# Scores from stacked high and low parts, and three norms in a written-out order

## What is computed

```python
# after the experts (L0_ffn), y is the attention's normed output
z = _layer_norm(y + _moe(y, ...), g2, be2)        # norm 0, with gain and shift
x = x + _layernorm(z)                             # norm 1
# second attention (L1_attn), called on _layernorm(x)
xn = _ln(_layernorm(x), g1, b1)                   # norm 2
q = _lin(xn, Wq, bq).reshape(b, n, 16, 8) / sqrt(8)
k = _lin(xn, Wk, bk).reshape(b, n, 16, 8)
score = softmax(einsum('bihd,bjhd->bhij', q, k))
v = _lin(xn, Wv, bv).reshape(b, n, 8, 8)
out = einsum('bhij,bjrd->bihrd', score, v)        # 8 values per head
comp = softmax(concat([qv, out]) @ Ws.T + bs, axis=3)
out = (comp * out).sum(axis=3)                    # 128 features per token
```

## Time and profile before

| | us |
|---|---|
| median of 3 runs (1008.1 to 1018.52) | 1008.54 |
| profiled execution | 1008.61 |
| its span, first to last instruction | 1006.9 |
| PE busy | 742.9 (74%) |
| DVE busy | 589.5 (59%) |
| ACT busy | 446.8 (44%) |
| POOL busy | 84.6 (8%) |

### The profile page before, as it was taken

How to read it: one execution, slowest core, us unless ns; L and a number is a source line. 1 busy time by engine, 2 the same in 40 slices (tenths; PEclk the granted TensorE clock), 3 DMA queues, 4 the chain that set the end, 5 groups by cost and what they waited for, 6 DMA issues and landing times. The chain is left out here.

```text
span 1006.9 us, 15707 instructions
## 1 busy us (share of the span) xinstructions
PE 742.9 (74%) x5853; PEld 608.8 (60%) x5853; DVE 589.5 (59%) x1330; ACT 446.8 (44%) x920; POOL 84.6 (8%) x96
## 2 busy tenths in 40 slices
PE   3993869998932695518940479999999974759986
PEld 2443769995432475418840347888888864538765
DVE  4119999983484363413327543777777657575574
ACT  3332526453534454203534614555555533446554
POOL 0002203000001101061420020000000001000000
PEclk9996757697955788557985569999999986869989
DMA  5200260005001000021020030000000000000000
GB/s 166 33 0 1 41 105 1 1 3 220 26 1 64 1 1 1 1 68 46 31 63 0 0 118 1 2 2 1 0 1 1 2 1 1 0 1 1 1 22 21
DMA packets 27457, 26.43 MB, mean 26 GB/s; under 512 B 17424, under 2 KB 25488, under 8 KB 26624
## 3 DMA queue, kind: packets, MB, share of 16 engines
q1 hardware_dynamic: 26144, 22.99, 8.0%
q0 software_dynamic: 1248, 2.57, 0.8%
HBM read 20.32 MB, written 5.23 MB: 25 GB/s over the span
## 5 line engine op out<-in xcount | busy, mean ns | idle before, releaser
L2201 PE MATMUL PS<-VXT,PT 128*128 128x73 f32 (+1 forms) x1024 | 126.6, 277 | 4.8 <-ACT PT L2225 4.8
L2201 PEld LDWEIGHTS PS<-VXT,PT 128*128 128x128 f32 x1024 | 119.7, 192 | 17.0 <-issue 12.3
L2312 DVE TENSOR_REDUCE MX<-PS 128x2 f32<-128x512 f32 x128 | 81.7, 686 | 47.5 <-PE PS L2164 46.8
L2225 ACT ACTIVATE PT<-PS 128x512 f32<-128x512 f32 x128 | 68.6, 597 | 47.4 <-PE PS L2169 47.4
L2161 PE MATMUL PS<-Q,KZ 32*128 32x256 f32 x512 | 76.8, 397 | 0.0
L2164 PE MATMUL PS<-KZ,Q 32*128 32x256 f32 x512 | 72.8, 409 | 1.9 <-DVE MX L2312 1.7
L2169 PE MATMUL PS<-MR,SEL 32*128 32x256 f32 x256 | 58.8, 462 | 0.0
L2238 ACT ACTIVATE UB<-PS 128x292 f32<-128x292 f32 x64 | 26.6, 415 | 52.8 <-PE PS L2201 52.8
L2164 PEld LDWEIGHTS PS<-KZ,Q 32*128 32x128 f32 x512 | 45.1, 190 | 5.3 <-DVE MX L2312 4.1
L404 PE MATMUL PS<-XT,WT 128*128 x96 | 42.3, 595 | 1.0 <-ACT XT L290 1.0
L2161 PEld LDWEIGHTS PS<-Q,KZ 32*128 32x128 f32 x512 | 38.8, 184 | 5.7 <-issue 0.8
(11 more groups left out here) (465 smaller groups left out, 1778.3 us busy)
## 6 DMA issues: line engine op xcount, KB each, us to landing
PB<-in_pb SPq DMA_DIRECT2D x1, 5016.0 KB, 17.7
PB<-in_pd SPq DMA_DIRECT2D x1, 2888.0 KB, 9.8
X<-in_x SPq DMA_DIRECT2D x2, 1024.0 KB, 4.8
X<-fir_rows SPq DMA_DIRECT2D x2, 1024.0 KB, 6.5
TR<-fir_rows SPq DMA_DIRECT2D x2, 1024.0 KB, 8.7
PA<-in_pa SPq DMA_DIRECT2D x1, 1731.0 KB, 8.5
PC<-in_pc SPq DMA_DIRECT2D x1, 1560.0 KB, 6.4
by_expert<-ZERO_ SPq DMA_DIRECT2D x1, 1483.5 KB, 15.7
```

What stands on the lines that cost most here:

```text
L2201: last = nc.tensor.matmul(PS[:, UM.bank(n), col:col + VX], PT[:, k % 4, c, f * P:(f + 1) * P], v, start=(c == 0), stop=(c == 1))
L2225: nc.scalar.activation(PT[:, k % 4, :, :], PS[:, UM.bank(n), :].rearrange("p (c q) -> p c q", c=2), ACT.Exp).then_inc(c_act, 1)
L2312: nc.vector.tensor_reduce(MX[:, :, k], PS[:, UP_.bank(n), :].rearrange("p (f q) -> p f q", f=2), AX.X, ALU.max, negate=True).then_inc(p_dv ...
```

## The change

1. **Queries and keys as high and low parts.** The projection is taken in two halves of another precision: ACT writes the fp32r-rounded high part (`high_parts`, two applies), DVE the rest (`low_parts`, two operations). For each group of 32 rows the four planes (query high, query low, key high, key low) are spread by 32 DMAs of 32 KB from SP (`spread`) into Q4 and K4, so that one head has, under one another in 32 rows, 8 rows each of high and low queries against high and low keys. One fp32r matmul over 32 rows then adds all four products. Q4 and K4 are kept three times, HALVES once. The weights' columns are laid out as "p (j d s)", and bias columns are permuted by a matmul with PERM.
2. **The attention's turns.** The hardware loop is gone: all turns are written out. The projection of batch b+2 moves to iteration 0 of turn b, right behind its scores, in the third slot of the maxima's rotation (SPLIT_BANK, bank 2), and the low parts to DVE's iteration 1. PE's next use of that bank (the sixth maximum, in `scores(2)`) waits for both parts. The maxima of the next turn wait for the spread of their batch, and ACT's high parts for the spread before.
3. **The applies into OB** leave norm 2; the 16 of them stand behind the high parts of batch 1, before turn 0.
4. **The three norms** follow an order written out per engine, one (k, g) at a time; `end(k, g)` now ends with `begin(k + 1, g)`. Batch 0 is split there, between `turned(1)` and `apply(2, 2)` on ACT and behind `middle(2, 3)` on DVE, and SP's part of the block ends with `spread(0)`.
5. At the block's beginning DVE makes the permuted bias columns behind SEL and PE multiplies them with PERM, between its gain columns and the product with BD; some bias arithmetic after the fold gets shorter.

The diff, cut to its core:

```diff
+        def high_parts(act, bank, b):
+            act.wait_ge(split_full, b + 1)
+            if b:
+                arrived(act, b - 1)
+            for s_ in range(2):
+                nc.scalar.activation(HALVES[:, 2 * s_, :], bank[:, s_ * L:(s_ + 1) * L], ACT.Identity,
+                                     bias=BS[:, s_:s_ + 1]).then_inc(split_high, 1)
+
+        def low_parts(dve, bank, b):
+            dve.wait_ge(split_high, 2 * b + 2)
+            for s_ in range(2):
+                nc.vector.scalar_tensor_tensor(out=HALVES[:, 2 * s_ + 1, :], in0=bank[:, s_ * L:(s_ + 1) * L],
+                                               scalar=BS[:, s_:s_ + 1], in1=HALVES[:, 2 * s_, :], op0=ALU.add,
+                                               op1=ALU.subtract).then_inc(split_low, 1)
+
+        def spread(sp, b):
+            sp.wait_ge(split_high, 2 * b + 2)
+            sp.wait_ge(split_low, 2 * b + 2)
+            for to, plane_of in ((Q4, lambda c: c // 2), (K4, lambda c: 2 + c % 2)):
+                for g in range(4):
+                    for c in range(4):
+                        at = 32 * g + 8 * c
+                        sp.dma_start(to[b % 3][at:at + 8, :, :].bitcast(F32),
+                                     HALVES[32 * g:32 * g + 32, plane_of(c), :].bitcast(F32)).then_inc(split_in[b % 4], 16)
...
+                    pe.wait_ge(c_bias, 1)
+                    pe.wait_ge(c_perm, 1)
+                    nc.tensor.matmul(PS[:, 3, 8:10], PERM[:, :], BC[:, :],
+                                     start=True, stop=True)
                     pe.wait_ge(c_bd, 1)
...
+                    begin(0, 0)
+                    begin(0, 1)
+                    middle(0, 0)
+                    begin(0, 2)
+                    middle(0, 1)
+                    begin(0, 3)
+                    end(0, 0)
+                    middle(0, 2)
+                    end(0, 1)
+                    middle(1, 0)
+                    end(0, 2)
+                    middle(0, 3)
+                    end(1, 0)
+                    middle(1, 1)
+                    end(0, 3)
+                    middle(2, 0)
+                    middle(1, 2)
+                    end(1, 1)
+                    middle(1, 3)
+                    end(1, 2)
+                    middle(2, 1)
+                    end(1, 3)
+                    middle(2, 2)
+                    values(0)
+                    middle(2, 3)
+                    low_parts(dve, PS[:, 0, :], 0)
+                    values(1)
+                    values(2)
+                    values(3)
...
-            prep = ROUND + [("qk", 0), ("turn", 0)]
+            prep = ROUND[0:2] + [("qk", 0)] + ROUND[2:] + [("turn", 0)]
...
+                for b in [None] + list(range(B)):
+                    after = 0 if b is None else b + 1
+                    last = after == B
                     for i in range(H2 // 2):
+                        scores(i, b, None if last else after)
+                        if i == 0 and after + 1 < B:
+                            project_next(after + 1)
+                        if i == 1 and after + 1 < B:
+                            split_next(after + 1)
...
+                    for b in range(1, B):
+                        if b >= 3:
+                            UM.wait_full(sp, b - 3, at_m[("exp", H2 - 1)])
+                        spread(sp, b)
...
+                                nc.tensor.matmul(PS[:, UM.bank(at_m[("exp", k)]), os], K4[b % 3][rows_of(k), k // 4, cs],
+                                                 Q4[b % 3][rows_of(k), k // 4, :], start=True, stop=False)
...
+                        if b == 1:
+                            for t in range(NT):
+                                nc.scalar.activation(XL[:, t, :], X[:, t, :], ACT.Identity, bias=NMG[:, 0, t:t + 1],
+                                                     scale=R2S[:, 0, t:t + 1])
```

More of the change, by code:

```diff
@@ L1724, in build @@
             sba.close()
+            SPLIT = sr.enter_context(nc.sbuf_tensor("SPLIT", [P, 7, 4, L], F32R, side="right"))
+            Q4, K4 = ([SPLIT[:, 2 * n + s_, :, :] for n in range(3)] for s_ in range(2))
+            HALVES = SPLIT[:, 6, :, :]
             XBT = sbuf(sb, "XBT", [P, SLOTS * P])
@@ L1913, in _ @@
+                    turned(3)
                 @block.vector
```

282 lines of the change are left out of this document (135 added, 147 removed).

## The result

| | us |
|---|---|
| the kernel before, median of 4 executions | 1009.24 |
| the changed kernel, median of 4 executions (1113.84 to 1132.9) | 1120.38 |
| ratio, 95% interval | 1.106, 1.100 to 1.112 |
| its profiled execution, and its span | 1132.9, 1131.2 |
| forecast (range) | 987 (977 to 1008) |

What follows compares the result with a forecast made beforehand. PE was taken to bound the attention, while no engine was full in the norms. Gains 12.6 (earlier turn 0) + 11.2 (turns) - 2.2 (experts) = 21.6 us off span 1006.9 give 985.3, plus 1.7 around it 987 us; range 977 to 1008.

Steps and rivals of the forecast that it cites:

- the clock falls in the loop: Rival: PE's new waits in the attention turns lower its clock, +15 us, 1002 us (998 to 1012); chance 0.15.
- Step 1: Attention's score block on PE: cheaper matmuls take it from 1.30 to 0.70 us, bounds 0.60 and 0.90.
- Step 2: Full attention turn: DVE decides, 26.6 us against 26.78, so turns 1 to 5 gain only 0.7 us.
- A: Stretch of a full turn from scores(0) to scores(2), behind DVE's low parts: 6.3 us, before 4.57.
- PE's saving comes through: Rival: full attention turns fall to about 24.6 us, 10 us more gained, 976 us; chance 0.09.
- Step 3: The other attention turns: turn 0 gains 4.1 us, turn 6 2.3, turn 7 4.1; 11.2 together with turns 1 to 5.
- Step 4: Norms behind the experts: new order ends the last values at 45.5 instead of 61.1 us, gain 15.6.
- T: Clock reading of the forecast's norms and attention start: time in us counted from 522.7 in the old profile.
- Step 5: Spread DMAs on SP: 0.40 us per issue (0.33 to 0.51), 3.1 us of the norms' gain lost, turn 0 12.6 earlier.
- SP becomes the bound: Rival: SP's DMA issue sets the attention turn, kernel slower, 1045 us at 0.75 us per issue; chance 0.12.
- d: SP's issue time per spread DMA; above 0.58 us the spread passes the full turn, at 0.61 all gain is gone.
- Step 6: Experts' start: PE waits for DVE's bias columns, costing 2.2 us, bounds 0.5 and 3.

Runs made afterwards that it cites:

- e13: Changed kernel with transfers issued by SyncE and GpSimd, exponential table loaded early, applies into OB on GpSimd, low parts ahead of the "start" steps; ratio 1.050 to before.
- e5: Changed kernel with DMAs for batch 0 only, every batch reading batch 0's copies (wrong scores); 1099.8 us.
- e8: Changed kernel with the transfers of batches 1 to 7 issued half by SyncE, half by GpSimd; 1101.4 us.
- e10: Kernel before with norms' new order, applies into OB on GpSimd, early exponential table load, one-pass Q and KZ without low parts; 985.9 to 1015.7 us.
- e17: e13 with two plain 512-column products ahead of PE's wait for the stabilizers in turns 1 to 6; ratio 1.011 to before.
- e1: Kernel before with only the norms' new order and the applies into OB moved to ACT ahead of turn 0; 1019.4 us, ratio 1.007.
- e12: e4 with each score product issued four times into the same place; 1115.3 us.
- e3: Changed kernel with DMAs for batches 0, 1 and 2 only, later batches reading those again (wrong scores); 1122.5 us.
- e2: Kernel before with only Q and KZ kept as one-pass floats, no low parts, less precise scores; 1061.1, 1045.4, 1035.6 and 1015.7 us.
- e4: Changed kernel with eight plain products behind the wait for batch 1's transfers, in place of four ahead of it; 1129.4 us.
- e7: e2 with each score product issued twice into the same place; 1024.9 to 1058.1 us.
- e18: e10 with each score product of the last turn issued four times; median 1031.4 us, best 978.8 us.
- e15: e10 with four dummy copies on ACT ahead of turn 5's first exponential, to lengthen PE's gap there; 1014.4 us.
- e11: e5 with each score product issued four times into the same place; 1098.7 us.

## Why the prediction was wrong

**The step that failed is the rival "the clock falls in the loop".** It named the mechanism and a right place (e13 lost the clock at the wait for M4, e5 and e8 at the wait before scores(2)), and then priced it as an incident: "double weighted(7) and the next scores: some 2 to 3 us in six turns, +15", chance 0.15. That takes for granted that the clock comes back once PE is busy. Measured: it stays at 0.50 for the rest of the loop, with PE busy 25.00 of 25 us, at 13.5 us a turn and some 117 us in the loop and behind it. The forecast doubled two pieces only, but a fall lengthens *every* piece of PE's work, and in before's loop that is all but 0.4 us of 25. What the trace of before could not show was how the light block behaves at 0.50; there was a bound for it, an estimate from before's rows (PE's work per turn, 26.4 less 8 x 0.6, doubled: 43 us, so 8 x 16 = 130 us if it never comes back), and the range should have reached for it. The sum itself put the clock at nothing: it counted each new wait of PE as its own length, or less.

**Step 1, the score block: right.** 0.66 us at full clock (638.54 to 639.20 in e5), 0.70 forecast (its own terms add up to 0.68).

**Step 2, the full turn: its terms came out, where a run shows them.** A was forecast at 6.3; e5 shows 6.17 from scores(0) at 636.82 to scores(2) at 642.99. From scores(2) to the "end" steps 3.5 was forecast, ending on ACT's CM; e10 shows 3.46 with that wait (630.63 to 634.09). From there to M4's end 14.5 was forecast, and it is 14.28 in e10 (to 648.37) and in e13 (638.59 to 652.87). With 2.2 for the rest that gives 26.1 us for a full turn in the order of the change at full clock, an estimate from these rows, for the 26.6 forecast; no run shows such a turn whole. The 24.5 us of e13 and 24.4 of e17 are not the rival "PE's saving comes through" (24.6, chance 0.09): there the low parts stand ahead of the "start" steps, A is 4.32 (630.60 to 634.92) and the part behind it 18.10 (to 653.02), as forecast (18.0). The order of two groups of DVE's work is worth 1.6 to 1.9 us a turn (26.1 against 24.5; 6.17 against 4.32). "PE loses 0.6 us of work eight times a turn and turns nearly all of it into waiting" was right as well, and it is just what brought the clock down: the forecast priced the waits at nothing because the turn was no longer PE's.

**Step 3: right for turn 0.** From scores(0) to scores(0) it takes 23.1 us in e5 (613.70 to 636.82), 22.7 forecast. It was 28.1 before (608.51 to 636.60), so the gain is 5.0 and not 4.1, which was reckoned against a full turn; by MR's copies it is 4.3 (30.7 to 26.4). Turns 6 and 7 were never seen at full clock in this loop.

**Step 4, the norms: right.** Low parts end at T 35.1 (35.8 forecast), the last values at T 44.2 (45.5). As an edit by itself it gives 13.7 to 15.3 us up to the first copy of MR.

But "where ACT has nothing to do during the first reductions; if that cover were gone they would cost up to 7.7" was checked for the changed kernel alone, and there for its own time only: in e1 the applies reach past the cover, PE waits 2 us longer, the clock falls, and the turn is 18 us longer.

**Step 5, the spread: the price of an issue was wrong.** 0.714 us against 0.40, and above the upper bound of 0.51 (the lower one, 0.33, stands in no row; 0.36 is the least there). Smaller DMAs were not cheaper to issue. spread(0) ends at T 58.0 instead of 48.6. The block's end waits for SyncE, PE idles, batch 1's copies land at T 93.6, and turn 0 starts 7.8 us later than before, not 12.6 earlier. The rival "SP becomes the bound" was right in its condition (d over 0.58) and near in the length of its turn: e12 shows 32.4 to 34.2 us for 6.3 + 32 x 0.714 + 2 = 31.1. At full clock it would have given 1036 by the forecast's own sum; it decides nothing here, since a turn at half clock is longer still (e3).

**Step 6: 3.7 us** for the longer start of the experts' block (from the load of their tokens to the norms 76.9 us against 73.2), 2.2 forecast, bound 3.

**What is shown and what is not.** Shown: the loss is for the most part the clock at 0.50 in the loop, with some 20 us for the transfers; the light block alone makes the clock fall and stay down for turns (e2); filling one of PE's waits gives the clock back for most of the loop (e17 against e13, where nothing else changes), and closing one goes with it (e10 against e2, which differ in the norms' order besides). The dense loop outlived 1.73 and 1.77 us and came back by itself from longer waits (e1, e12). The light one fell behind single waits of 0.66 to 2.4 us and then mostly stayed down for turns (in e2, e4, e7 and e18 it came back for more than a few us, after 115 to 230 us). Not shown: a rule by which a given gap decides. Waits of 0.87 and 0.88 us ended differently (e4, e5), and so did 1.08 and 1.09 (both in e15). Nor is it shown that density alone is the reason: two products for each score held the clock no better than one (e7), and dense work fell and stayed down as well, in e11 from turn 5 on and in the last turns of e12.

## What to carry over

When PE is the bound and its work gets cheaper, first ask whether it will still be without gaps: it becomes an engine that waits, and its clock is a second, larger term than the work saved. Price a fall of the clock for the whole rest of the loop, not for the stretch in which it falls. Look for PE's longest single waits (a table load, a reordered helper, a moved apply, a wait put in for a reused bank) and close them, or fill them with plain products, before the cheaper block goes in; and time such a kernel in many executions, since one good execution (978.8 us) says little.

## What was not expected of the hardware

- PE busy 313.66 of 315 us (630 to 945) in the changed kernel, and granted 0.50 throughout. The Trainium skill, "TensorE: Matmul & The Clock Gate", "Part 1: The HAM clock gate", says that "activity releases the throttle". If activity is read as the profile's busy time, this trace does not agree: 230.00 of 230 us busy (630 to 860) released nothing.
- SyncE takes 0.714 us to issue a DMA of 32 KB in 32 rows, GpSimd 0.546; four larger ones took 0.36 to 0.51. The two issue side by side: in e8 batch 1's copies are there 14.8 us after SyncE's first issue of them (601.29 to 616.07), in the changed kernel 25.2 us after it (601.74 to 626.98).
- A DVE cast of 0.18 us lasted 5.36 us while GpSimd ran 5.39 us of fp32r casts (e17), and a DVE product of 2.0 us lasted 6.11 beside the same casts (e8); DVE's reductions beside them kept their length.
- The load of ACT's exponential table, 1.28 us, in front of a loop's first exponential cost PE a gap of 1.7 us; one dummy exponential in the prologue takes it away (0.45).
